# Layer 0: weights ahead of the mixing, in float32r with 384 columns, and longer lead for normalisation and statistics

## What is computed

```python
adj_0 = jnp.diag(jnp.diagonal(adj))
adj_1 = jnp.triu(adj, k=1)
adj_2 = jnp.tril(adj, k=-1)
h = jnp.einsum('bjf,kfo->kbjo', x, W)
out = jnp.einsum('ij,bjo->bio', adj_0, h[0]) + jnp.einsum('ij,bjo->bio', adj_1, h[1]) + jnp.einsum('ij,bjo->bio', adj_2, h[2])
return out + bias[None, None, :]
```

## Time and profile before

| | us |
|---|---|
| median of 3 runs | 1301.64 (1301.43 to 1303.98) |
| the profiled execution | 1302.56 |
| its span, first to last instruction | 1300.8 |
| busy in the span: PE, DVE, ACT, POOL | 1233.4, 1018.0, 869.3, 327.2 |
| layer 0 in the span | 30.42 to 201.35 |

### The profile page before, as it was taken

One profiled execution on the slowest core, in us unless ns is written; L12 is line 12 of the kernel. 1 busy time (PEld: TensorE's weight loads), 2 busy tenths in 40 slices (PEclk: granted clock), 3 DMA queues, 4 the chain that ended last, 5 costly groups with the idle time before them and its releaser, 6 DMA issues.

```text
span 1300.8 us, 23507 instructions
## 1 busy us (share of the span) xinstructions
PE 1233.4 (95%) x7340; PEld 1024.8 (79%) x7340; DVE 1018.0 (78%) x2039; ACT 869.3 (67%) x1649; POOL 327.2 (25%) x738
## 2 busy tenths in 40 slices
PE   2999999999999998899999999999999899988998
PEld 1989996664388887689778887988897778768998
DVE  4788766996768885998788878887876699986664
ACT  1666657867758886877687768777766677752332
POOL 3577761000057440000000000000000566642331
PEclk9999999999999999999999999999999999998999
DMA  8000000000031110000000000002100300001112
GB/s 302 1 0 0 0 0 0 0 1 0 0 131 66 71 57 1 1 1 1 1 1 1 1 1 1 1 1 81 49 1 1 130 1 2 1 2 41 66 74 82
DMA packets 14475, 38.02 MB, mean 29 GB/s; under 512 B 1856, under 2 KB 3904, under 8 KB 13120
## 3 DMA queue, kind: packets, MB, share of 16 engines
q1 hardware_dynamic: 13008, 36.31, 7.3%
q10 hardware_dynamic: 1392, 0.74, 0.2%
HBM read 20.27 MB, written 16.78 MB: 28 GB/s over the span
## 4 chain that ended last, share of the span: by engine, by line
PE 52%; DVE 5%; ACT 2%; issue 1%; POOL 1%; POOLq 0%; DVEq 0%; ACTq 0%
PE bank L966 7%; PE bank L967 7%; PE bank L968 7%; PE bank L1546 5%; PE bank L981 4%; PE bank L1334 4%; PE bank L1346 4%; PE bank L977 4%; PE bank L978 4%; PE bank L1536 2%; PE bank L1554 2%; ACT gates L996 1%; PE bank L1318 1%; PE bank L1239 1%; DVE Y L1051 1%
## 5 line engine op out<-in xcount | busy, mean ns | idle before, releaser
L996 ACT ACTIVATE gates<-bank,lstm_bias 128x512 f32<-128x512 f32 (+1 forms) x504 | 301.9, 637 | 101.4 <-PE bank L981 88.3
L150 ACT ACTIVATE l_h<-X,nmr,rstd 128x128 f32 (+1 forms) x512 | 209.9, 483 | 56.7 <-POOLq L144 36.0
L966 PE MATMUL bank<-lstm_node_hi,Wih_hi 128*128 128x512 f32 (+1 forms) x408 | 149.5, 366 | 0.0
L967 PE MATMUL bank<-lstm_node_hi,Wih_lo 128*128 128x512 f32 (+1 forms) x408 | 148.9, 365 | 0.0
L968 PE MATMUL bank<-lstm_node_lo,Wih_hi 128*128 128x512 f32 (+1 forms) x408 | 148.8, 365 | 0.0
L119 POOL TENSOR_TENSOR l2r_sum<-l2r_st 128x8 f32<-128x8 f32 x16 | 4.2, 265 | 528.8 <-DVE l2r_st L100 528.8
L977 PE MATMUL bank<-lstm_hid_hi,Whh_hi 128*128 128x512 f32 (+1 forms) x288 | 104.1, 362 | 3.9 <-DVE lstm_hid_hi L1056 3.8
L981 PE MATMUL bank<-lstm_hid_lo,Whh_hi 128*128 128x512 f32 (+1 forms) x288 | 106.8, 371 | 0.0
L978 PE MATMUL bank<-lstm_hid_hi,Whh_lo 128*128 128x512 f32 (+1 forms) x288 | 103.1, 358 | 0.0
L1001 ACT ACTIVATE gates<-lstm_cell 128x512 f32<-128x512 f32 (+1 forms) x144 | 83.7, 581 | 20.8 <-DVE lstm_cell L1043 20.4
L968 PEld LDWEIGHTS bank<-lstm_node_lo,Wih_hi 128*128 128x128 f32 x408 | 77.1, 189 | 11.7
(11 more groups left out here) (247 smaller groups left out, 3279.8 us busy)
## 6 DMA issues: line engine op xcount, KB each, us to landing
X<-in_x SPq DMA_DIRECT2D x8, 1024.0 KB, 14.6
x_spill<-X SPq DMA_DIRECT2D x32, 256.0 KB, 2.0
X<-x_spill SPq DMA_DIRECT2D x2, 4096.0 KB, 12.7
out<-X SPq DMA_DIRECT2D x32, 256.0 KB, 2.0
w_raw<-in_WihT SPq DMA_DIRECT2D x1, 1024.0 KB, 6.4
w_raw<-in_WhhT SPq DMA_DIRECT2D x1, 1024.0 KB, 8.9
W<-in_L_W ACTq DMA_DIRECT2D x1, 192.0 KB, 4.9
rows<-in_rows ACTq DMA_DIRECT2D x1, 128.0 KB, 3.9
```

The costliest lines, as they stand in the source:

```text
L150: last = act.activation(h[:, j, :], k.X[:, bass.ds(b0, TB), :][:, j, :], ACT.Relu, bias=k.nmr[:, bass.ds(b0, TB)][:, j:j + 1], scale=k.rst ...
L966: pe.matmul(out, hi, x_high, start=True, stop=False)
L967: pe.matmul(out, lo, x_high, start=False, stop=False)
L996: act.activation(gate_of(it, g), k.bank[4 * s + g][:, 0:it.N], ACT.Tanh if g == GATE_G else ACT.Sigmoid, bias=k.lstm_bias[:, it.p - 1, g:g ...
```

## The change

Layer 0 works in the other order. Each transposed tile (hT, rounded to hT_hi by ACT and to hT_lo by DVE, straight out of PSUM) is multiplied with all three weights side by side: three float32r products of 384 columns for each batch, into psH, four banks of PSUM, one for each batch of a tile. ACT copies psH to H in two instructions of 768 elements. The mixing over nodes is then done for four batches in one float32 product of 512 columns for each triangle; the diagonal part is a scalar_tensor_tensor on DVE with the diagonal as a column, added to X. The weights are split into W_hi and W_lo on DVE at the start.

The streams of ACT, PE and DVE are written in steps of one tile instead of turns of two: in step t, transpose t + 1, products of t, mixing of t - 1; ACT normalises tile t + 3. Seven steps ahead of the loop and eight behind it are written out. X_AHEAD goes from 2 to 3; the edge stage waits for the second load of x and takes three turns of x statistics. POOL's code is the same. In the setup a product and its copy (the diagonal along rows) give way to a copy of one column. The banks of PSUM become slices of one tensor.

```diff
-    bank_dg, bank_di = k.bank[0], k.bank[1]
+    bank_di = k.bank[1]
...
-            pe.wait_ge(deg, 1)
-            pe.matmul(bank_dg[:, 0:P], onesPP[:, :], tmp[:, :], start=True, stop=True).then_inc(diag_ready, 1)
...
+            dve.wait_ge(deg, 4)
+            dve.tensor_copy(k.diag_col[:, :], rs[:, 2:3])
             dve.wait_ge(diag_ready, 1)
-            dve.tensor_copy(k.diag_bc[:, :], bank_dg[:, 0:P])
-            dve.wait_ge(diag_ready, 2)
...
+    hT_hi, hT_lo = (each(S, lambda s: sb(f"l0_{n}{s}", [P, TB, P], F32R)) for n in ("hT_hi", "hT_lo"))
+    H = each(S, lambda s: sb(f"l0_H{s}", [P, 3, TB, P]))
+    W_hi, W_lo = (sb(f"l0_{n}", [P, 3, P], F32R) for n in ("W_hi", "W_lo"))
...
+    psT, psO = k.bank[0:2], k.bank[6:8]
+    psH = k.psum[:, 2 * TW:6 * TW].rearrange("p (j c) -> p j c", j=TB)
...
+    FIRST = -3
+
+    def steps(eng, step):
+
+
+        for t in range(FIRST, 2 * S):
+            step(t // S, t % S, t)
+        with eng.Fori(2, n_it - AHEAD) as i:
+            for s in range(S):
+                step(i, s, i * S + s)
+        for t in range(tiles - AHEAD * S, tiles + 2):
+            step(t // S, t % S, t)
...
-            def normalise(i):
-                for s in range(S):
-                    x_ln.wait(act, s, i)
-                    normalise_tile(act, k, h[s], (i * S + s) * TB).then_inc(h_ready[s], 1)
-                    act.wait_ge(h_ready[s], i + 1)
-                    act.activation(h_hi[s][:, :, :], h[s][:, :, :], ACT.Copy).then_inc(hi_ready[s], 1)
-
-            def turn(i, ahead):
-                for s in range(S):
+            def step(i, s, t):
+                q, ahead = (s + 1) % S, i + (s + 1) // S
+                if there(t + 1):
+                    act.wait_ge(T_ready[q], ahead + 1)
+                    act.activation(hT_hi[q][:, :, :], as_tile(psT[q]), ACT.Copy).then_inc(hi_ready[q], 1)
+                if there(t):
                     act.wait_ge(AB_ready[s], i + 1)
-                    act.activation(Z12[s][:, 0:2, :, :], psA[s][:, :], ACT.Copy)
-                    act.activation(Z12[s][:, 2:4, :, :], psB[s][:, :], ACT.Copy).then_inc(Z12_ready[s], 1)
-                if ahead:
-                    normalise(i + 1)
-
-            normalise(0)
-            looped(act, n_it, turn)
+                    if since(t, S):
+                        act.wait_ge(out_ready[s], i)
+                        act.wait_ge(H0_added[s], i)
+                    for j in range(0, TB, 2):
+                        last = act.activation(H[s][:, :, j:j + 2, :], psH[:, j:j + 2, 0:3 * P].rearrange("p j (k o) -> p k j o", k=3),
+                                              ACT.Copy)
+                    last.then_inc(H_ready[s], 1)
+                if there(t + 3):
+                    turn = i + (s + 3) // S
+                    x_ln.wait(act, q, turn)
+                    normalise_tile(act, k, h[q], (t + 3) * TB).then_inc(h_ready[q], 1)
+
+            steps(act, step)
...
-            pe.wait_ge(A_ready, 2)
-            with pe.Fori(0, n_it) as i:
-
-                for s in range(S):
-                    pe.wait_ge(h_ready[s], i + 1)
+            def step(i, s, t):
+                q, ahead = (s + 1) % S, i + (s + 1) // S
+                if there(t + 1):
+                    pe.wait_ge(h_ready[q], ahead + 1)
+                    if since(t + 1, S):
+                        pe.wait_ge(lo_ready[q], ahead)
                     for j in range(TB):
-                        last = pe.transpose(psT[s][:, j * P:(j + 1) * P], h[s][:, j, :], k.ident[:, :])
-                    last.then_inc(T_ready[s], 1)
+                        last = pe.transpose(psT[q][:, j * P:(j + 1) * P], h[q][:, j, :], k.ident[:, :])
+                    last.then_inc(T_ready[q], 1)
+                if there(t):
                     pe.wait_ge(lo_ready[s], i + 1)
+                    if since(t, 1):
+                        pe.wait_ge(H_ready[(s + 1) % S], i - (s + 1) % S + 1)
                     for j in range(TB):
-                        out = (psA, psB)[j // 2][s][:, (j % 2) * 2 * P:(j % 2 + 1) * 2 * P]
-                        pe.matmul(out, h_hi[s][:, j, :], A_hi[:, :, :], start=True, stop=False)
-                        pe.matmul(out, h_hi[s][:, j, :], A_lo[:, :, :], start=False, stop=False)
-                        last = pe.matmul(out, h_lo[s][:, j, :], A_hi[:, :, :], start=False, stop=True)
+                        o = psH[:, j, 0:3 * P]
+                        pe.matmul(o, hT_hi[s][:, j, :], W_hi[:, :, :], start=True, stop=False)
+                        pe.matmul(o, hT_hi[s][:, j, :], W_lo[:, :, :], start=False, stop=False)
+                        last = pe.matmul(o, hT_lo[s][:, j, :], W_hi[:, :, :], start=False, stop=True)
                     last.then_inc(AB_ready[s], 1)
-
-                for s in range(S):
-                    pe.wait_ge(Z0_ready[s], i + 1)
-                    pe.wait_ge(Z12_ready[s], i + 1)
-                    for j in range(TB):
-                        o = psO[s][:, j * P:(j + 1) * P]
-                        pe.matmul(o, Z0[s][:, j, :], k.W0[:, 0, :], start=True, stop=False)
-                        pe.matmul(o, Z12[s][:, j, 0, :], k.W0[:, 1, :], start=False, stop=False)
-                        last = pe.matmul(o, Z12[s][:, j, 1, :], k.W0[:, 2, :], start=False, stop=True)
-                    last.then_inc(out_ready[s], 1)
+                if there(t - 1):
+                    at = i - (s + 1) % S
+                    pe.wait_ge(H_ready[q], at + 1)
+                    if since(t - 1, S):
+                        pe.wait_ge(updated[q], at)
+                    pe.matmul(psO[q][:, :], k.A12T[:, 0, :], H[q][:, 0, :, :], start=True, stop=False)
+                    pe.matmul(psO[q][:, :], k.A12T[:, 1, :], H[q][:, 1, :, :], start=False, stop=True).then_inc(out_ready[q], 1)
+
+            pe.wait_ge(W_ready, 2)
+            steps(pe, step)
...
-            def h_low(i, s):
-                dve.wait_ge(hi_ready[s], i + 1)
-                dve.tensor_tensor(h_lo[s][:, :, :], h[s][:, :, :], h_hi[s][:, :, :], ALU.subtract).then_inc(lo_ready[s], 1)
-
-            def turn(i, more, following=True):
-                for s in range(S):
-                    dve.wait_ge(T_ready[s], i + 1)
-                    dve.tensor_tensor(Z0[s][:, :, :], psT[s][:, :].rearrange("p (b n) -> p b n", b=TB),
-                                      k.diag_bc[:, :].unsqueeze(1).broadcast_to([P, TB, P]),
-                                      ALU.mult).then_inc(Z0_ready[s], 1)
-
-                    dve.tensor_tensor(tile(i, s), tile(i, s), k.rows[:, R_L0:R_L0 + 1, :].broadcast_to([P, TB, P]),
+            def step(i, s, t):
+                q, ahead = (s + 1) % S, i + (s + 1) // S
+                if there(t + 1):
+                    dve.wait_ge(hi_ready[q], ahead + 1)
+                    dve.tensor_tensor(hT_lo[q][:, :, :], as_tile(psT[q]), hT_hi[q][:, :, :].bitcast(F32),
+                                      ALU.subtract).then_inc(lo_ready[q], 1)
+                if there(t):
+                    dve.tensor_tensor(tile(t), tile(t), k.rows[:, R_L0:R_L0 + 1, :].broadcast_to([P, TB, P]),
                                       ALU.add).then_inc(biased[s], 1)
-                if more:
-                    k.x_stats(dve, i + AHEAD)
-                for s in range(S):
-                    if following:
-                        h_low(i + 1, s)
+                if there(t - 1):
+                    at = i - (s + 1) % S
+                    dve.wait_ge(out_ready[q], at + 1)
+                    dve.wait_ge(H0_added[q], at + 1)
+                    dve.tensor_tensor(tile(t - 1), as_tile(psO[q]), tile(t - 1), ALU.add).then_inc(updated[q], 1)
+                    dve.wait_ge(updated[q], at + 1)
+                    ln.stats(dve, tile(t - 1), q, at)
+                if there(t) and there(t + AHEAD * S):
+                    k.x_ln.stats(dve, tile(t + AHEAD * S), s, i + AHEAD)
+                if there(t):
+                    dve.wait_ge(H_ready[s], i + 1)
                     dve.wait_ge(biased[s], i + 1)
-                    dve.wait_ge(out_ready[s], i + 1)
-                    dve.tensor_tensor(tile(i, s), psO[s][:, :].rearrange("p (b n) -> p b n", b=TB), tile(i, s),
-                                      ALU.add).then_inc(updated[s], 1)
-                for s in range(S):
-                    dve.wait_ge(updated[s], i + 1)
-                    ln.stats(dve, tile(i, s), s, i)
-
-            split_float32(dve, k.A12T[:, :, :], A_hi[:, :, :], A_lo[:, :, :], A_ready, 1).then_inc(A_ready, 1)
-            for s in range(S):
-                h_low(0, s)
+                    dve.scalar_tensor_tensor(tile(t), H[s][:, 2, :, :], k.diag_col[:, :], tile(t),
+                                             ALU.mult, ALU.add).then_inc(H0_added[s], 1)
...
+            W = k.W0
+            for n, part in enumerate((1, 2, 0)):
+                last = dve.tensor_copy(W_hi[:, n, :], W[:, part, :])
+            last.then_inc(W_ready, 1)
```

(42 more changed lines are left out.)

## The result

The changed kernel takes 1307.61 us (median of 8 runs, 1305.13 to 1310.22), the kernel before 1301.70 in the same runs. The ratio is 1.0044, with a 95% interval of 1.003 to 1.0057: slower by 0.44%. The forecast was 1307.0.

A forecast was written before the change was run, and what follows sets the result against it. POOL's back-to-back batches were taken to pace layer 0. Next stage at 52.4 + 12 x 10.4 + 5.1 + 24.5 = 206.8 us against 201.35, so +5.4 on 1301.6: 1307.0 us, range 1297 to 1315.

The forecast's parts named there:

- POOL's first batch after that: Fill of layer 0: POOL's first x batch comes 17.0 us after the start, at 52.4 us against 40.28.
- steady turn: Layer 0, two tiles of four batches: 9.64 + 0.4 + 0.4 = 10.4 us, bounds 9.64 and 11.1.
- thirteenth x batch to next stage: End of layer 0: coefficients ready after 5.1 us, then 24.5 us to the next stage.
- Pace: Layer 0: POOL's back-to-back batches set the turn, 10.13 us before the change; PE is 8% behind.
- Rival 3: Layer 0: PE is the floor, not POOL, 8.66 us a turn; about 1294 us; chance 0.07.
- Rival 4: Layer 0: PE's clock falls back, or a colder fill and three hits a turn; 1315 us; chance 0.13.
- Hits: Layer 0: DVE instructions with two SBUF operands stretch POOL's instructions twice a turn, about 0.4 us each.
- turn without hits: Layer 0: POOL's turn with no instruction held up by DVE, 10.13 - 0.49 = 9.64 us.
- rival 1: Layer 0: POOL paces, but one hit a turn, 10.13 us, or a fill 3 us shorter; 1303.8 us; chance 0.20.
- rival 2: Layer 0: no hit in most turns, 9.64 us a turn; 1297.9 us; chance 0.15.
- Edge stage: Before layer 0: third x_stats waits for POOL's second batch and delays DVE's edge chain; +5.0 us, bounds 3.0 and 7.
- The later stages do not change.: Stages behind layer 0: no change in time, 0 us.

The follow-up runs named there:

- after_again: The changed kernel unaltered, traced in a second series beside other kernels: 1307.75 us, ratio to the kernel before 1.0040.
- e3: The changed kernel with the third x statistics of the edge stage moved behind the edge weights' product on DVE: 1304.67 us, ratio to before 1.0013.
- e7: As e3, with POOL's third x batch also moved from the edge stage to the start of layer 0: 1303.06 us, ratio to before 1.0005.
- e2: The kernel before with POOL's pow in layer 0 replaced by a multiplication of the same size: 1289.25 us, ratio to before 0.9892.
- e1: The changed kernel with POOL's pow in layer 0's batches replaced by a multiplication of the same size: 1287.72 us, ratio to before 0.9886.
- e4: The changed kernel without the bias add on DVE: 1302.56 us, ratio to before 0.9998.
- e6: The changed kernel with POOL's coefficients made for four tiles at a time, x statistics eight tiles ahead: 1290.86 us, ratio to before 0.9909.
- e5: The changed kernel with X_AHEAD back at 2, statistics two turns ahead: 1402.38 us in one execution.

## Why the prediction was right

| step | forecast | measured |
|---|---|---|
| first x_stats, wait for x_in[1] | +0.3 | 16.68 against 15.93, +0.75 |
| third x_stats starts | 23.4 | 23.79 |
| start of layer 0 | 35.4 | 36.03 |
| POOL's first batch after that | 17.0 | 17.2 |
| products of 384 columns at 2.4 GHz | 0.18 each | 0.18 (108.41 to 108.59) |
| the same at 1.2 GHz | 12 in 3.9 | 0.32 each, 12 in 4.0 |
| mixing | 1.72 | 1.72 (110.16 to 111.88) |
| steady turn | 10.4 | 10.06; 10.17 over 12 turns (the first two 11.06 and 10.31) |
| thirteenth x batch to next stage | 29.6 | 30.32 (175.29 to 205.61) |
| next stage starts | 206.8 | 205.61 |
| layer 0's loss, with the edge stage's | +5.4 | +4.26 |
| the stages behind it | 0 | +2.1; +1.0 in after_again |

The products at either level of the clock and the mixing in PE's timeline of the changed kernel, against the earlier trace rows:

```profile
41.06 0.52 PE L368 MATMUL psum<-l_W_lo,l_hT_hi 128*128 128x384 f32 x1
...
41.38 0.52 PE L369 MATMUL psum<-l_W_hi,l_hT_lo 128*128 128x384 f32 x1
...
108.41 0.35 PE L369 MATMUL psum<-l_W_hi,l_hT_lo 128*128 128x384 f32 x1
...
108.59 0.34 PE L367 MATMUL psum<-l_W_hi,l_hT_hi 128*128 128x384 f32 x1
...
110.16 1.02 PE L376 MATMUL psum<-l_H,A12T 128*128 128x512 f32 x2
...
111.88 0.60 PE L359 MATMUL psum<-ident,l_h 128*128 128x128 f32 x4
```

**Pace.** Right: POOL, not PE, sets the turn. The two runs with a short pow and the one without the bias add show it from both sides. PE's sum was right too: 8.66 us a turn, and 8.57 where the short pow lets PE pace. Rival 3 (PE is the floor) fell. So did, as a guide to this stage, the rule of the Trainium skill (Perfetto Trace Analysis, Identifying the Most-Contended Engine) that the engine of highest occupancy is optimised first. The section judges TensorE by its weight loads rather than by its products; that makes 90% here (9.15 of 10.13 us) instead of 92%, and the choice is the same. PE's products got 5.5 us of relief over the stage and its weight loads 41 us (154.19 to 113.01), and nothing came of it, while the engine with 70% occupancy was the one to shorten. Rival 4 (the clock) fell in this stage: the granted clock is 1.00 from 50 to 180 us.

**Hits.** Right in number and place: one at the start of the x batch's pow, behind the scalar_tensor_tensor (+0.34, forecast 0.4), one at the l batch's rstd, behind the bias add (+0.29, forecast 0.4). The contention that the Trainium skill names (GPSIMD Engine Reference, Key points) is worth 0.63 us a turn here. DVE waits at the l statistics only, not at the x statistics as forecast, but the phases are the expected ones all the same: the bias add starts 2.8 us after the second l_diff, forecast 2.8 to 3.4. Mis-sized was the turn without hits: 9.64 was taken from 10.13 less one hit of 0.49. The changed kernel gives 10.06 - 0.34 - 0.29 = 9.43, and 0.16 us of the difference are in the gap ahead of x_sum, 0.76 us before and 0.60 after. This is no further hit of a DVE instruction. In an earlier turn of the kernel before, the gap (52.58 to 53.39) is 0.81 us long, and DVE idles for nearly all of it; timelines of POOL and DVE:

```profile
53.39 0.68 POOL L119 TENSOR_TENSOR x_sum<-x_st 128x8 f32<-128x8 f32 x1 [0.81 <-POOL nmr L119]
...
53.31 0.69 DVE L369 TENSOR_TENSOR l_h_lo<-l_h,l_h_hi 128x512 fp32r<-128x512 f32 x1 [0.92 <-ACT l_h_hi L323]
```

What makes the gap longer there stays open. The forecast's sum, 10.44, is 0.38 us above the measured turn: 0.21 by this base, 0.17 by hits of 0.63 instead of 0.8. The turn came out nearest to the 10.13 of rival 1, though by two hits on a shorter base and not by one hit; rival 2 (no hit) is out.

**Edge stage.** Right in mechanism: x_stats(2) behind POOL's second batch, the chain queued behind it. Its size was 5.61 for 5.0: the load of x was worth 0.75 and not 0.3, setup's 0.12 included, and what follows the chain's start 0.40 (5.61 less the 5.21 from 20.13 to 25.34) and not 0.2. The e3 and e7 runs confirm that this delay is, within the error, the whole of the loss.

**What came out equal by luck.** Layer 0's loss was forecast 1.1 us too large. What makes up for it is the step that was put at nothing without a reason: "The later stages do not change." Their instructions are the same, but in the traces they take longer. From the start of the next stage to the end of the span the kernel before has 1099.5 us and e2, of the same order, 1099.0. The kernels of the new order have 1101.6 (the changed kernel), 1100.5 (after_again), 1101.7 (e1), 1103.0 (e3), 1100.1 (e4), 1101.6 (e6) and 1100.5 (e7); e5 alone, with 1099.2, does not. So the hit of the forecast to 0.6 us is partly luck.

In the changed kernel 1.9 of the 2.1 us arise between 985 and 1038 us. The windows of 20 us at the start of the scores (a part of the last layer), before:

```profile
1022.20:1042.20 20.00, 18.18 (x118) 13.90 (x117) 16.10 (x34) 13.26 (x29) 14.35 (x31) 1.00 0.38 160
```

and after, at the same place in the work, 3.9 us later:

```profile
1026.10:1046.10 20.00, 17.90 (x100) 12.72 (x99) 14.38 (x32) 12.31 (x27) 13.48 (x29) 0.91 0.37 159
```

The granted clock is 1.00 in the one and 0.91 in the other, in the same part of the work. In e7 1.5 us arise near 540 us, where a window of 20 us (526 to 546) reads 0.91 and that of the kernel before at the same work (528.5 to 548.5) reads 1.00. But such a dip does not always cost time: after_again has one too (0.94 from 1006.6 to 1026.6), and that stretch is longer by 0.2 us only. That the dips make the whole of the 1 to 2 us, and why the new order should have more of them, was not shown; runs of the changed kernel scatter by 0.4% (1305.13 to 1310.22), and each kernel but the changed one has a single trace.

## What to carry to other kernels

Before an engine is relieved, look whether its partners' batches start behind their own last instruction: an engine that is 70% busy with dependent small instructions can set the pace, and making the busiest engine faster then buys only waits. A longer lead costs its preparation; with one buffer for the statistics the third set had to wait for the consumer of the second, and everything queued behind it on that engine was late, one for one to the end of the layer. What gained here was halving the number of dependent rounds (a wider batch), not less work for the engine that looked full. And stages that the change does not touch are worth a look in the traces of every variant: here they took 0.6 to 3.5 us more than before in seven traces of eight, where 6 us were to be explained.

## What the runs showed of the hardware

A POOL pow on 8 columns takes 1.64 us and on 16 columns 2.91; an ordinary instruction 0.20 and 0.22. A window at the start of layer 0 in the changed kernel reads a granted clock of 1.00:

```profile
40.00:42.00 2.00, 1.81 (x6) 1.43 (x5) 0.76 (x2) 1.72 (x5) 0.00 (x0) 1.00 0.00 0
```

Its products of 384 columns start 0.32 us apart there (41.06 to 41.38), and 0.18 later. In e7 the same products, again 0.32 us apart (34.85 to 35.17), stand in a window that reads 0.50:

```profile
34.00:36.00 2.00, 1.81 (x6) 1.64 (x6) 0.77 (x2) 1.51 (x4) 0.40 (x3) 0.50 0.00 0
```

So 0.32 us is their spacing at 1.2 GHz, and the 1.00 of the changed kernel is not a reading: the records of the granted clock in its trace begin at 45.8 us only, and the column shows 1.00 where there is none. At the start of a trace the spacing of the products, not the column, tells the level.
